# A graph layer with indirect gathers: seven tiles of source rows gathered row by row by SP, partly inside the node stage

## The reference

```python
h = maximum(layernorm(x, axis=-1), 0)              # x: 100000 x 32
w = silu(silu(edge_attr_8 @ W1 + b1) @ W2 + b2) @ W3 + b3   # 25000 edges, 256 weights each
hs, hv = h[src][:, :8], h[src][:, 8:].reshape(-1, 8, 3)
m0 = ALPHA * (einsum(hs * sh0, w00) + INV_SQRT3 * einsum(hv . sh1, w110))
m1 = ALPHA * (einsum(hs, sh1, w01) + einsum(hv * sh0, w10))
agg = segment_sum([m0, m1], dst, 100000) / 4       # dst is sorted
out = x + [h_scalars @ Ws, h_vectors @ Wv] / sqrt(8) + agg
```

## Time and profile before

| | |
|---|---|
| median of three runs | 644.88 us (643.75 to 645.25) |
| the profiled execution | 641.12 us |
| its span, first to last instruction | 639.3 us |
| mean granted clock of PE | 0.82 of full speed |
| HBM | 17.6 MB read, 16.1 MB written |

### The profile page before, as it was taken

One profiled execution on the slowest core, in us unless ns is written; L12 is line 12 of the kernel. 1 busy time (PEld: TensorE's weight loads), 2 busy tenths in 40 slices (PEclk: granted clock), 3 DMA queues, 4 the chain that ended last, 5 costly groups with the idle time before them and its releaser, 6 DMA issues.

```text
span 639.3 us, 11923 instructions
## 1 busy us (share of the span) xinstructions
PE 527.2 (82%) x2867; PEld 393.4 (62%) x2867; DVE 464.0 (73%) x1126; ACT 388.3 (61%) x1104; POOL 500.9 (78%) x396
## 2 busy tenths in 40 slices
PE   6799999989589899898989889899888987059730
PEld 4688887778256667666666666576656664037530
DVE  4799986777389978777778877787777784069910
ACT  3355555455387858667576867577675777038900
POOL 6777777777777888888888888888888888638886
PEclk9899999898697877686888887867777888558955
DMA  4866665553110122222222222222222222202222
GB/s 125 254 190 207 196 207 175 162 162 114 53 15 15 13 11 11 11 10 11 9 12 9 11 11 12 10 10 11 9 11 9 12 10 10 8 3 10 10 8 8
DMA packets 51881, 34.26 MB, mean 54 GB/s; under 512 B 35382, under 2 KB 39288, under 8 KB 51832
## 3 DMA queue, kind: packets, MB, share of 16 engines
q0 software_dynamic: 34336, 6.37, 18.7%
q1 hardware_dynamic: 17432, 27.35, 12.4%
q10 hardware_dynamic: 64, 0.00, 0.0%
HBM read 17.58 MB, written 16.08 MB: 53 GB/s over the span
## 4 chain that ended last, share of the span: by engine, by line
POOL 59%; issue 21%; DMA 15%; SPq 2%; DVE 2%; POOLq 0%; DVEq 0%
POOL out_dram L333 38%; POOL xg L316 21%; DMA out_dram<-sums,idx_i 14%; DMA xin<-in_x_dram 1%; DVE oc L822 1%; DMA wself<-in_L_gnn_Wv_dram 0%; SPq L237 0%; SPq L257 0%; DVE oc L829 0%; SPq L218 0%; DVE nsum L791 0%; SPq L232 0%; SPq L251 0%; SPq L252 0%; SPq L250 0%
## 5 line engine op out<-in xcount | busy, mean ns | idle before, releaser
L333 POOL DMA_INDIRECT out_dram<-sums,idx_i x196 | 305.7, 1560 | 76.0 <-issue 52.3
L316 POOL DMA_INDIRECT xg<-in_x_dram,src_all x191 | 194.2, 1017 | 59.7 <-issue 57.3
L637 PE MATMUL ps<-w3blk,x 128*128 128x512 f32 x196 | 137.1, 789 | 0.0
L691 PE MATMUL ps<-msg,eq 128*128 128x32 f32 (+1 forms) x980 | 128.7, 291 | 1.6 <-DVE msg L1026 1.1
L691 PEld LDWEIGHTS ps<-msg,eq 128*128 128x128 f32 x980 | 128.2, 213 | 1.9 <-DVE msg L1026 1.8
L1006 DVE TENSOR_REDUCE red<-prod 128x128 f32<-128x1024 f32 x49 | 97.7, 1994 | 0.1
L467 ACT ACTIVATE sums<-ps 128x132 f32<-128x132 f32 x49 | 13.7, 279 | 134.6 <-POOLq L343 90.1
L479 ACT ACTIVATE dsq<-ps,dcol 128x512 f32<-128x512 f32 x196 | 87.1, 536 | 0.2 <-PE ps L649 0.2
L501 ACT ACTIVATE eq<-dsq,onecol 128x384 f32<-128x384 f32 x147 | 73.4, 518 | 0.0
L637 PEld LDWEIGHTS ps<-w3blk,x 128*128 128x128 f32 x196 | 45.8, 248 | 43.5 <-issue 40.1
L649 PEld LDWEIGHTS ps<-ident,dcol 128*128 128x128 f32 x196 | 25.0, 151 | 61.6 <-issue 59.4
(11 more groups left out here) (103 smaller groups left out, 836.3 us busy)
## 6 DMA issues: line engine op xcount, KB each, us to landing
xin<-in_x_dram SPq DMA_DIRECT2D x48, 256.0 KB, 3.2
out_dram<-oc SPq DMA_DIRECT2D x48, 256.0 KB, 2.1
xg<-in_x_dram SPq DMA_DIRECT2D x552, 0.1 KB
out_dram<-sums,idx_i POOLq DMA_INDIRECT x196, 3.1
xg<-in_x_dram,src_all POOLq DMA_INDIRECT x191, 2.4
er_all<-in_edge_attr_dram SPq DMA_DIRECT2D x1, 780.0 KB
sh_all<-in_edge_attr_dram SPq DMA_DIRECT2D x1, 390.0 KB
xin<-in_x_dram SPq DMA_DIRECT2D x1, 192.0 KB
```

The lines of the kernel that those rows point to most:

```text
L316: pool.indirect_dma_start(xg[:, t * D:(t + 1) * D], None, x, bass.IndirectOffsetOnAxis(ap=src_all[:, t:t + 1], axis=0)).then_inc(signal, 16)
L333: pool.indirect_dma_start(out, bass.IndirectOffsetOnAxis(ap=idx_i[:, k % NS, a:a + 1], axis=0), sums[:, k % NS, a * DR:a * DR + D], None, ...
L637: pe.matmul(o, x2[:, k // 2 % 2, j * P:(j + 1) * P], w3blk[:, :], start=True, stop=False)
L691: m = pe.matmul(psSUM[:, a * DR:a * DR + n], eq[:, k % 2, o:o + P], msg[:, k % 2, b, 0:n], start=(b == a), stop=(b == a - 1 and (a < BT - ...
```

## The change

- SP gathers seven tiles (RT = 7): 6 x 128 + 40 = 808 rows. G1 falls from 191 to 189, so POOL gathers two tiles fewer.
- The numbers of these rows come into one partition (row_i), by seven small strided loads; the load into src_all's last column, its memset and the semaphore of each are gone.
- SP's node stage is written out, without a loop. Behind the pair of each chunk from 8 to 47 stand six rows (240 in all); the other 568 follow the last store. The order is tile by tile. The numbers are loaded into registers sixteen at a time.
- The sums of the last late tiles move from pass 10 (batch 42) to the start of pass 11 (batch 44), and their other feature steps, on ACT and DVE, with them.
- Group 0 of POOL's gathers has its own semaphore, and group 2 doesn't wait for gsum any more.

```diff
-    GT, GL, GA, RT = 10, 7, 157, 5
+    GT, GL, GA, RT = 10, 7, 157, 7
@@
+        row_i = sb("row_i", [1, RT * P], i32)
@@ sync
-            sp.wait_ge(src_pad, 1)
-            sp.dma_start(src_all[0:TAIL, T:T + 1], src_tail).then_inc(srclast_loaded, 16)
@@
+            for t in range(G1, T + 1):
+                n = P if t < T else TAIL
+                rows_of = src_main[:, t:t + 1].rearrange("p a -> a p") if t < T else src_tail.rearrange("n a -> a n")
+                with nc.allow_non_contiguous_dma(reason="128 row numbers"):
+                    sp.dma_start(row_i[:, (t - G1) * P:(t - G1) * P + n], rows_of).then_inc(row_loaded, 16)
@@
-            node_pass(0, True)
-            with sp.Fori(1, DLOOP - 1) as i:
-                node_pass(i, False)
-            for k in range(DBODY):
-                c = (DLOOP - 1) * DBODY + k
+            late_rows = iter([(t, p) for t in range(G1, T + 1) for p in range(P if t < T else TAIL)])
+            nodes = []
+
+            def gather_rows(count):
+
+                for t, p in itertools.islice(late_rows, count):
+                    if p % 16 == 0:
+                        o = (t - G1) * P + p
+                        w = min(16, (P if t < T else TAIL) - p)
+                        _, numbers = nc.values_load_multi_w_load_instructions(
+                            row_i[0:1, o:o + w], engines=[mybir.EngineType.SP], min_val=0, max_val=N - 1,
+                            skip_runtime_bounds_check_because="src holds rows of x")
+                        nodes[:] = numbers
+                    sp.dma_start(xg[p:p + 1, t * D:(t + 1) * D], x[ds(nodes[p % 16], 1), :])\
+                      .then_inc(gathered_row[t - G1], 16)
+
+            sp.wait_ge(row_loaded, 16 * RT)
+            for c in range(XS, NCH):
                 store(c - XS, c - XS)
                 load_x(c, c)
-            for c in range(FULL, NCH):
-                store(c - XS, c - XS)
-                load_x(c, c)
+                if c < FULL:
+                    gather_rows(6)
             for c in range(NCH - XS, NCH):
                 store(c, c)
-            sp.wait_ge(srclast_loaded, 16)
-            for p in range(P):
...
+            gather_rows(P * RT)
@@ gpsimd
-                if n >= 2:
+                if n >= 3:
                     pool.wait_ge(s["gsum_done"], n - 1)
@@ vector, edge_pass
-                        if h == 1 and r == 0 and not last:
+                        if h == 1 and r == 0 and v < LATE - 1:
                             late_landed(v)
                             feat_sum(n, t0, GL)
+                        if h == 0 and r == 0 and last:
+                            late_landed(v - 1)
+                            feat_sum(n - 1, was, GL)
```

More of the change, by code:

```diff
@@ L14 @@
+import itertools
 import numpy as np
@@ L191, in gnn_layer @@
         stored = [sem(f"stored{i}") for i in range(XS)]
-        src_loaded, src_pad, srclast_loaded = sem("src_loaded"), sem("src_pad"), sem("srclast_loaded")
-        gathered = [sem(f"gathered{i}") for i in range(2)]
+        src_loaded, row_loaded = sem("src_loaded"), sem("row_loaded")
+        gathered = [sem(f"gathered{i}") for i in range(3)]
         gathered_late = [sem(f"gathered_late{i}") for i in range(LATE)]
@@ L314, in gather @@
             def gather(t):
-                signal = gathered[t // GT % 2] if t < GF else gathered_late[(t - GF) // GL]
+                signal = gathered_late[(t - GF) // GL] if t >= GF else gathered[t // GT % 2 if t >= GT else 2]
                 pool.indirect_dma_start(xg[:, t * D:(t + 1) * D], None, x,
@@ L512, in _, with edge_pass @@
             mlp_two(1, 1)
-            def edge_pass(v, first, last):
+            def edge_pass(v, first, last, squares):
                 n = EARLY + v
@@ L524, in edge_pass @@
                     dst_square(q + 1, kq + 1)
-                    if h == 0:
+                    if h == 0 and not last:
                         feat_std(n - 1, GT if first else GL)
@@ L530, in edge_pass @@
                     dst_equal(q + 1, kq + 1)
-                    if h == 1 and not last:
+                    if h == 1 and squares:
                         feat_square(n, GL)
+                    if h == 0 and last:
+                        feat_square(n - 1, GL)
                     copy_sums(q, kq)
@@ L537, in edge_pass @@
                         dst_col(q + 4, kq + 4)
+                    if h == 0 and last:
+                        feat_std(n - 1, GL)
                     dst_equal(q + 2, kq + 2)
[L540 to L543, removed]
+            edge_pass(0, True, False, True)
+            with act.Fori(1, LATE - 1) as v:
+                edge_pass(v, False, False, True)
+            edge_pass(LATE - 1, False, False, False)
+            edge_pass(LATE, False, True, False)
             copy_sums(NQ - 2, NQ - 2)
@@ L886, in node_step @@
                     odd = base % 8 == 2
-                    dve.wait_ge(gathered[odd], (i if odd else i + 1) * (16 * GT))
+                    if base < 8:
+                        dve.wait_ge(gathered[2], 16 * GT)
+                    else:
+                        dve.wait_ge(gathered[odd], i * (16 * GT))
                     feat_sum(n, n * GT, GT)
@@ L1062, in edge_pass @@
                         sum_vectors(q, k)
-                        if h == 1 and r == 0 and not last:
+                        if h == 1 and r == 0 and v < LATE - 1:
                             feat_centre(n, t0, GL)
+                        if h == 0 and r == 0 and last:
+                            feat_centre(n - 1, was, GL)
                         if ready:
                             index_later(q - 2, k - 2)
-                        if h == 0 and r == 0:
+                        if h == 0 and r == 0 and not last:
                             feat_var(n - 1, ww)
```

10 lines of the change are left out of this document (2 added, 8 removed).

## The result

The changed kernel takes 658.9 us (657.2 to 659.4, four runs), the kernel before beside it 644.3 us (642.1 to 645.3): a ratio of 1.0227 with an interval of 1.0193 to 1.0260. The forecast was 682.3 us. The sign is right; of the 37.4 us of loss that were forecast, 14.5 came in the medians.

A forecast was written before the change was run, and what follows sets the result against it. POOL's gathers and scatters, and what makes POOL wait, were taken to bound the kernel. Group 11 53.4 us later less 16.0 gained behind the first scatter gave +37.4 on 644.9: 682.3 us, range 650 to 697.

The forecast's parts named there:

- The load of numbers: SP's register load of sixteen row numbers: 3.6 us, from 0.207 us for each number beyond five at 1.358 us.
- Rival 1: SP loads sixteen numbers as fast as five, 1.36 us; group 11 21.7 us late, +5.7, 650.6 us; chance 0.08.
- SP's other terms: SP's node stage: first pair at 30 us, 0.87 us for a pair, 0.41 us for a row.
- The chain from SP to POOL: Node stage: load 43 delays DVE's sums and, through gsum, POOL's group 11, 7.0 us behind; nine waits, some 50 us.
- The gain behind the first scatter: POOL's first scatter to the end: 16.0 us less, 2.2 from two gathers and 13.8 from the idx_i stall.
- The late rows: SP's 568 rows behind the node stage land by 610; DVE waits some 9 us, 16 are covered, POOL's stall goes.
- The sum: Whole kernel: 53.4 us later group 11 less 16.0 gained, +37.4 us on 644.9, giving 682.3 us.
- the main case: Whole kernel: 682.3 us with number loads between 3.1 and 4.1 us; own range 670 to 695, chance 0.78.
- Rival 2: SP's load of sixteen numbers costs under 1 us, so the kernel gets faster; at 0.6 us 639.8 us; chance 0.06.
- its break-even: SP's load of sixteen at 0.96 us: POOL's group 11 may come 16.0 us late before the change costs anything.

The follow-up runs named there:

- the probe: The changed kernel with 120 more register loads on SP behind its last row, 1 to 16 numbers from different start words; 696.6 us.
- the later features alone: The kernel before with only the last feature steps on ACT and DVE moved from batch 42 to 44; 636.4 us, ratio 0.9855.

## Why the prediction was right in its sign and wrong in its size

- **The load of numbers** is the step that failed: "I take 3.6: it is the only slope the trace has, and the two kinds of load differ in nothing else I can see". Measured 1.23. Over the 14 loads ahead of load 43 this is 14 x 2.37 x 1.013 = 33.6 us too much. The two kinds did differ in nothing else; what was not asked is what they had in common, a first word at 191, and the change's lists, which begin at multiples of sixteen, don't share it. The slope was right for them (0.20 in the probe) and was carried to a list of another kind. Rival 1, with 1.36 us and 650.6 us, had this price nearly right and got a chance of 0.08.
- **SP's other terms.** The first pair came at 31.4 for 30, and a row took 0.44 for 0.41 us beside the node stage, over 210 rows 5.7 us; the pair held at 0.87. Load 43: 200 + 1.8 - 33.6 + 5.7 = 173.9, against 173.34. Rival 1 had +5.7 where the profiles have +18.3: 5.0 of the 12.6 us are in group 11 (175.3 against 180.3), 4.5 between it and the first scatter (58.6 against 63.1, mostly the misread row below), 3.1 in the gain.
- **The chain from SP to POOL** was right: 7.0 us from load 43 to group 11 (173.34 to 180.31), nine waits for gsum, 34.6 us in all for the forecast's 50. Raising the price of the loads moved the time as the chain says. Removing the wait freed POOL's gathers as it says, but gained at most 8 us.
- **A misread row.** "Group 11 therefore starts at 30 + 170 + 7 = 207, not at 153.63": 153.63 is the fourth gather of group 11 of the kernel before; its first is at 149.86. That made the delay 3.8 us too small. In the profiles: forecast delay of group 11 53.4, load 43 26.7 earlier than forecast, 3.8 for the misreading: 30.5, measured 30.45.
- **The gain behind the first scatter** was forecast at 16.0 and is 12.9. The starts of the batches show where the 3 are (a step is the time from one batch's first scatter to the next one's). The step with the stall took 20.91 us, 13.3 more than the 7.65 of the others without a gather, and two steps fewer have a gather, 2.3: that makes 15.5. But the 17 steps without a gather take 7.79 us on average in the change, where the 14 others of before took 7.65, which gives 2.3 back, and those with one 0.3. From the first scatter to the end four rows need 413.5 and, in the second run, 417.6 us, the odd word 414.8, the change in its second run 413.0: so the 417.8 of the later features alone, whose rows are 12.8 us late, is within what one kernel spreads over.
- **The late rows** were covered as forecast, and by more: SP's 568 rows took 281 us, 0.495 each, and ended 90 us before DVE asked.
- **The sum**: 37.4 - 22.2 (first scatter) + 3.1 (gain) = 18.3 between the profiled executions. The range, 650 to 697, held the time by way of rival 1, at its lower end: the main case's own range, 670 to 695, did not, so that is luck of the range and not of the working. Rival 2's condition, a load under 0.96 us, wasn't met, and its break-even was too kind. It rested on the misread row, on 0.41 for a row and on a gain of 16.0: with the numbers measured, six rows put group 11 at 31.8 + 35 x 0.87 + 210 x 0.443 + 7.0 = 162.3 even with loads at no cost, 12.4 later than before, against a gain of 12.9 (an estimate). Six rows would have been level at best. Five rows, with group 11 at 160.6, are at 0.996 the last count that is.

## What to carry to other kernels

Before a queue in a loop is given more to issue, add up its own time for a turn and compare it with the pace of the consumer: four rows at 2.95 us, under 3.03, cost nothing to be seen, and with six at 4.04 the kernel was 2.3% slower. Then ask what the added work brings: the kernel with four rows gained 1.7%, but the moved features alone gained 1.5%. A slope from two rows is a price only for what both have in common: ask what that is (here the place of the first word) before it is stretched from five to sixteen. Where a wait carries a delay to the bound engine, look for the next path behind it before hoping for its whole length: of 34 us of waiting for gsum, its removal gave 8 in one run and nothing in the other.

## What the runs showed of the chip that was not expected

- A register load on SP from SBUF takes four numbers for little more than one where its list begins at a multiple of sixteen words: 1 in 0.49, 4 in 0.52, 16 in 1.19 us. At an odd first word 4 take 1.09 and 16 take 3.48. Starts between the two kinds were not run. Moving the lists by one word cost this kernel 31 us (odd word, 689.8 against 658.9).
- From word 0, seven numbers take 1.15 us and eight 0.74: it pays to fill a load up to a full four.
- A single number takes 0.49 us, less than the floor of about 600 ns that the Trainium skill states (DMA: Bandwidth & Descriptors, section Latency and other measured facts).
- A row's DMA on SP takes 0.41 to 0.44 us of SP's time, with what stands ahead of it for its address. No slowing of POOL's gathers or of the loads of x by the traffic of such rows is seen: with 160 of them in the node stage the first scatter stood at 212.7 and 216.6, with none at 215.9, and loads of x landed in 3.4 and 3.0 us with them, in 3.4 with none.
- On one chip the node stage ran to 331 us in place of 169 for the same program (four rows), and the kernel before took 789.6 us; what slowed it there stays open.
